# Macaron block on one core: the opening loads most tokens behind the first routing weights, moves the low halves of the weights to POOL, and lets ScalarE normalise three groups whole

## The reference

```python
x = L0_attn_x                                        # (8, 1024, 128) float32
x = x + 0.5 * _L0_ffn_ref(_layernorm(x), Wg, bias_corr, W1, W2, Ws1, Ws2)
x = x + _L0_attn_ref(_layernorm(x), Qw, Kw, Vw)
x = x + 0.5 * _L0_ffn_ref(_layernorm(x), Wg, bias_corr, W1, W2, Ws1, Ws2)
```

```python
scores = sigmoid(flat @ Wg.T)                        # 16 experts in 4 groups
topk_idx, topk_w = _route(scores, bias_corr)         # best 2 groups, best 4 experts, weights normalised, x 2.5
hid = _relu2(einsum('th,eih->eti', flat, W1))        # 16 experts of 64 hidden units
y = einsum('eti,ehi->eth', hid, W2)
out = einsum('eth,te->th', y, cw) + _relu2(flat @ Ws1.T) @ Ws2.T
```

## Time and profile before

| | |
|---|---|
| median of 3 runs | 702.88 us (702.61 to 703.27) |
| profiled execution | 702.95 us |
| its span in the profile | 701.2 us |
| PE busy, of the span | 96% |
| DVE, ACT, POOL busy | 81%, 76%, 62% |
| feed-forward groups in a phase | 16 |

### The profile page before, as it was taken

The page is one execution under the profiler, slowest core; times in us unless marked ns, Lnnn a source line. Parts: engine busy times, 40 slices in busy tenths (PEclk is TensorE's granted clock), DMA queues, the critical chain, the costliest instruction groups (busy, mean ns, idle before and its releaser), DMA issues.

```text
span 701.2 us, 15091 instructions
## 1 busy us (share of the span) xinstructions
PE 673.3 (96%) x3367; PEld 527.5 (75%) x3367; DVE 567.5 (81%) x2586; ACT 529.6 (76%) x1094; POOL 438.2 (62%) x346
## 2 busy tenths in 40 slices
PE   4799999999999997999999999999999999999997
PEld 4567878888788875787778777778788887888775
DVE  5898998899888985666656678898988998889863
ACT  3578888888888866675566477659888788887875
POOL 3379888998889972000000021148889898898875
PEclk9999999999999999999999999999999999999999
DMA  9856776567765640000000000365776787767782
GB/s 246 196 124 138 162 165 145 124 147 154 162 143 123 152 90 0 1 1 1 0 1 0 0 0 1 71 134 115 158 166 140 166 179 171 165 139 174 166 178 72
DMA packets 53525, 78.37 MB, mean 112 GB/s; under 512 B 5216, under 2 KB 19184, under 8 KB 53488
## 3 DMA queue, kind: packets, MB, share of 16 engines
q1 hardware_dynamic: 51280, 77.36, 50.4%
q10 hardware_dynamic: 2208, 0.59, 0.4%
HBM read 72.70 MB, written 5.24 MB: 111 GB/s over the span
## 4 chain that ended last, share of the span: by engine, by line
PE 78%; DVE 10%; ACT 5%; issue 3%; POOL 1%; DMA 1%; POOLq 0%; DVEq 0%; ACTq 0%
PE psum L1188 18%; PE psum L1190 18%; PE psum L1189 18%; PE psum L1397 7%; PE psum L1227 4%; PE psum L1249 4%; DVE nmax L1068 3%; PE psum L1219 2%; PE psum L1261 2%; PE psum L1386 2%; ACT shared L611 2%; PE psum L1410 2%; DVE zn L1082 1%; DVE s_sb L939 1%; ACT wb L446 1%
## 5 line engine op out<-in xcount | busy, mean ns | idle before, releaser
L379 POOL TENSOR_TENSOR shared_r<-shared,shared_r 128x512 fp32r<-128x512 f32 x256 | 325.9, 1294 | 55.6 <-ACT shared L505 53.5
L939 DVE SCALAR_TENSOR_TENSOR s_sb<-psum,wb 128x512 f32<-128x512 f32 x256 | 175.5, 687 | 46.2 <-PE psum L1190 25.9
L505 ACT ACTIVATE shared<-s_sb 128x512 f32<-128x512 f32 x288 | 178.1, 620 | 28.6 <-DVE s_sb L939 28.6
L504 ACT ACTIVATE shared_r<-s_sb 128x512 fp32r<-128x512 f32 x256 | 159.8, 624 | 45.3 <-DVE s_sb L939 43.5
L1188 PE MATMUL psum<-x_hi,w_hi 128*128 128x512 f32 x288 | 127.2, 442 | 1.0 <-DVE x_sb L1094 0.5
L1190 PE MATMUL psum<-x_hi,w_lo 128*128 128x512 f32 x288 | 114.3, 397 | 0.0
L1189 PE MATMUL psum<-x_lo,w_hi 128*128 128x512 f32 x288 | 113.5, 394 | 0.0
L1188 PE MATMUL psum<-shared_r,w_hi 128*128 128x512 f32 x256 | 109.5, 428 | 0.8 <-POOL shared_r L379 0.7
L1189 PE MATMUL psum<-shared_r,w_hi 128*128 128x512 f32 x256 | 101.2, 395 | 0.0
L1190 PE MATMUL psum<-shared_r,w_lo 128*128 128x512 f32 x256 | 101.0, 395 | 0.0
L362 POOL TENSOR_TENSOR a_rstd<-a_mv,neg_half 128x8 f32<-128x8 f32 x8 | 13.1, 1636 | 116.4 <-DVE a_mv L758 116.4
(11 more groups left out here) (166 smaller groups left out, 1301.5 us busy)
## 6 DMA issues: line engine op xcount, KB each, us to landing
wb<-scratch SPq DMA_DIRECT2D x128, 512.0 KB, 8.3
out<-x_sb SPq DMA_DIRECT2D x16, 256.0 KB, 9.8
x_sb<-in_L_attn_x SPq DMA_DIRECT2D x4, 256.0 KB, 6.1
scratch<-wT SPq DMA_DIRECT2D x32, 32.0 KB, 1.9
w_raw<-in_L_ffn_W ACTq DMA_DIRECT2D x1, 512.0 KB, 5.8
w_raw<-in_L_ffn_W SPq DMA_DIRECT2D x1, 512.0 KB, 6.7
w_raw<-in_L_ffn_Ws ACTq DMA_DIRECT2D x1, 64.0 KB, 8.6
w_raw<-in_L_ffn_Ws SPq DMA_DIRECT2D x1, 64.0 KB, 7.2
```

The source lines that it names most:

```text
L379: nc.gpsimd.tensor_tensor(g_lo[:, j % RING, :], g_f[:, j % RING, :], g_hi[:, j % RING, :].bitcast(F32), ALU.subtract).then_inc(F.glo_done, 1)
L504: nc.scalar.activation(g_hi[:, j % RING, :], s_sb[:, j % RING, :], ACT.Square)
L505: nc.scalar.activation(g_f[:, j % RING, :], s_sb[:, j % RING, :], ACT.Square).then_inc(F.sq_done, 1)
L939: ins = nc.vector.scalar_tensor_tensor(s_, h_, 0.0, wb[:, u, c, :], ALU.max, ALU.mult)
```

## The change

It touches the opening alone, and the loads of tokens that belong to it.

- The first 4 tiles come in two DMAs, one from SP and one from ACT. ACT issues the loads of `W2` and `Ws2` only when both have landed.
- Group 4 has a DMA of its own, behind `Qw`, `Kw` and `Vw`. Groups 5 and 6 (512 KB) are issued behind the four `wb` loads of group 0, and groups 7 to 15 (2.36 MB) behind those of group 1. DVE waits for the former ahead of the loop's first body and for the latter ahead of the hardware loop.
- `weights_lo` goes from DVE to POOL. POOL can't read PSUM, so ACT writes an unrounded copy of each set as well (`wt_f`, in `zn` and `oT`).
- ACT normalises groups 1, 2 and 3 whole (four tiles in place of two), and DVE only makes their `shift`.
- PE gets 32 transposes of the identity whose result nobody reads (`keep_busy`), the first `w_transpose` goes ahead of the fourth set of weights, and PE waits for two low sets ahead of the first `up` and for all five ahead of the first `down`.

```diff
@@ block.sync
-            sp.dma_start(x_sb[:, 0:TG, :], x_v[:, 0:TG, :]).then_inc(x_in[0], 16)
+            sp.dma_start(x_sb[:, 0:TG // 2, :], x_v[:, 0:TG // 2, :]).then_inc(x_in[0], 16)
...
-            sp.dma_start(x_sb[:, 4 * TG:NT, :], x_v[:, 4 * TG:NT, :]).then_inc(x_rest, 16)
             sp.dma_start(qk_raw[:, 0, :], Qw).then_inc(small_in, 16)
             sp.dma_start(qk_raw[:, 1, :], Kw).then_inc(small_in, 16)
             sp.dma_start(vw[:], Vw).then_inc(small_in, 16)
+            sp.dma_start(x_sb[:, 4 * TG:5 * TG, :], x_v[:, 4 * TG:5 * TG, :]).then_inc(x_in[4], 16)
...
                 for n in range(2 * UN):
                     spread(n, n % UN)
+                    if phase == 0 and n < 2:
+                        cs = slice(TG * XR[n], TG * XR[n + 1])
+                        sp.dma_start(x_sb[:, cs, :], x_v[:, cs, :]).then_inc(x_rest[n], 16)
@@ block.gpsimd, start
                     if F is FF[0]:
                         x_lo_part(0, 0)
+                        weights_lo(0)
                         norm_root(0)
                         inv(2)
+                        weights_lo(1)
...
+                    if F is FF[0]:
+                        weights_lo(2)
+                    inv(3)
                     x_lo_part(1, 1)
-                    inv(3)
                     norm_root(1)
+                    if F is FF[0]:
+                        weights_lo(3)
+                        weights_lo(4)
@@ block.scalar
+            sc.dma_start(x_sb[:, TG // 2:TG, :], x_v[:, TG // 2:TG, :]).then_inc(x_in[0], 16)
+            sc.wait_ge(const_done, 1)
+            nc.scalar.activation(warm[:], neg_half[:], ACT.Sigmoid)
+            sc.wait_ge(x_in[0], 32)
             sc.dma_start(w2_raw[:, 0:NC, :].rearrange("h c (j i) -> h (c j) i", i=I),
...
                     sigmoid(0, 0, lg_ps)
-                    first_half(1)
+                    whole_group(1)
                     x_hi_copy(0, 0)
                     weights_hi(0)
                     x_copy(1, 1, tr_ps)
                     weights_hi(1)
                     sigmoid(1, 1, lg_ps)
                     weights_hi(2)
+                    wT_copy(0, wT_ps)
                     weights_hi(3)
                     x_hi_copy(1, 1)
-                    wT_copy(0, wT_ps)
-                    first_half(2)
+                    whole_group(2)
...
-                    first_half(3)
+                    whole_group(3)
@@ weights_hi
                 if w < 2:
-                    copy(flat(w1_hi, w), src).then_inc(wt_hi, 1)
+                    copy(flat(w1_hi, w), src)
+                    copy(wt_f[w], src).then_inc(wt_hi, 1)
@@ block.vector, opening
                     statistics(1)
-                    second_half(1)
+                    norm_shift(1)
...
-                    weights_lo(0)
-                    weights_lo(1)
-                    second_half(2)
+                    route_parts(1, 0, 1)
+                    norm_shift(2)
@@ block.tensor
+                def keep_busy(times):
+                    for n in range(times):
+                        nc.tensor.transpose(wt_ps[4][:, 0:P], ident[:], ident[:])
...
                     pe.wait_ge(const_done, 2)
+                    keep_busy(20)
                     pe.wait_ge(wg_in, 16)
                     nc.tensor.transpose(lg_ps[:, 0:E], wg_raw[:], ident[0:E, 0:E]).then_inc(wgT_done, 1)
+                    keep_busy(12)
...
                     pe.wait_ge(wt_hi, N_SETS)
-                    pe.wait_ge(wt_lo, N_SETS)
+                    pe.wait_ge(wt_lo, 2)
```

More of the change, by code:

```diff
@@ L222, in macaron_kernel @@
         uT = s_sb[:, AHEAD:AHEAD + 2, :]
+        zn_flat = zn[:].rearrange("p u t d -> p (u t d)")
+        wt_f = [zn_flat[:, 512 * w:512 * (w + 1)] for w in range(4)] + [oT[:]]
         psum = ctx.enter_context(nc.psum_tensor("psum", [P, 8, 512], F32))
@@ L256, in macaron_kernel @@
         N_SETS = len(wt_ps)
-        x_in = [sem(f"x_in{g}") for g in range(4)]
-        x_rest = sem("x_rest")
+        x_in = [sem(f"x_in{g}") for g in range(5)]
+        x_rest = [sem(f"x_rest{n}") for n in range(2)]
+        XR = (5, 7, NG)
         wg_in, bias_in, w1_in, w2_in, small_in = sem("wg_in"), sem("bias_in"), sem("w1_in"), sem("w2_in"), sem("small_in")
@@ L365, in attention_inv, with weights_lo @@
                 inv_std(AT, b, a_mv[:, :, 1], a_rstd[:], [(AT.zn_done, 2 * b)])
+            def weights_lo(w):
+                pool.wait_ge(wt_hi, w + 1)
+                flat = lambda a, k: a[:, 4 * k:4 * k + 4, :].rearrange("p c n -> p (c n)")
+                lo_of = lambda lo, hi, f: nc.gpsimd.tensor_tensor(lo, f, hi.bitcast(F32), ALU.subtract)
+                if w < 2:
+                    lo_of(flat(w1_lo, w), flat(w1_hi, w), wt_f[w]).then_inc(wt_lo, 1)
+                elif w < 4:
+                    lo_of(flat(w2_lo, w - 2), flat(w2_hi, w - 2), wt_f[w]).then_inc(wt_lo, 1)
+                else:
+                    lo_of(w1_lo[:, NC, :], w1_hi[:, NC, :], wt_f[w][:, 0:P])
+                    lo_of(w2_lo[:, NC, :], w2_hi[:, NC, :], wt_f[w][:, P:2 * P]).then_inc(wt_lo, 1)
             def ffn(F):
@@ L450, in _ @@
             sc.dma_start(w2_raw[:, NC, :], Ws2).then_inc(w2_in, 16)
-            sc.wait_ge(const_done, 1)
-            nc.scalar.activation(warm[:], neg_half[:], ACT.Sigmoid)
             def normalise(F, g, t):
@@ L509, in first_half, with whole_group @@
                         normalise(F, n, t)
+                def whole_group(n):
+                    for t in range(TG):
+                        normalise(F, n, t)
                 def opening():
@@ L688, in weights_hi @@
                             copy(w2_f[:, n, :], src[:, (c % 4) * P:(c % 4 + 1) * P])
-                    copy(flat(w2_hi, w - 2), src).then_inc(wt_hi, 1)
+                    copy(flat(w2_hi, w - 2), src)
+                    copy(wt_f[w], src).then_inc(wt_hi, 1)
                 else:
@@ L692, in weights_hi @@
                     copy(w2_hi[:, NC, :], src[:, P:2 * P])
+                    copy(wt_f[w][:, 0:2 * P], src[:, 0:2 * P])
                     copy(qkT[:].rearrange("p c n -> p (c n)"), src[:, 2 * P:4 * P]).then_inc(wt_hi, 1)
@@ L724, in _ @@
             v.wait_ge(FF[0].stat, n_const)
[L726 to L737, removed]
             def carry(place):
@@ L960, in statistics @@
                     def statistics(n):
-                        v.wait_ge(x_in[n], 16)
+                        v.wait_ge(x_in[n], 32 if n == 0 else 16)
                         stats(n, range(TG))
@@ L972, in opening @@
                     route_parts(0, 9)
-                    weights_lo(0)
-                    weights_lo(1)
-                    second_half(2)
+                    route_parts(1, 0, 1)
+                    norm_shift(2)
                     statistics(3)
[L977 to L980, removed]
-                    route_parts(1, 2)
-                    weights_lo(4)
-                    route_parts(1, 3, 4, 5, 6, 7, 8)
-                    v.wait_ge(x_rest, 16)
+                    route_parts(1, 2, 3, 4)
+                    norm_shift(3)
+                    route_parts(1, 5, 6, 7, 8)
+                    v.wait_ge(x_in[4], 16)
                     for c in range(AHEAD):
@@ L1040, in run @@
                 def run(first_extra, last_extra):
+                    if phase == 0:
+                        v.wait_ge(x_rest[0], 16)
                     body(0, True, False, first_extra)
+                    if phase == 0:
+                        v.wait_ge(x_rest[1], 16)
                     if phase == 1:
@@ L1246, in down @@
                         wait(pe, F.oT_copied, g - 1)
+                        if phase == 0 and isinstance(g, int) and g == 0:
+                            pe.wait_ge(wt_lo, N_SETS)
                     if c in WHOLE:
@@ L1277, in opening @@
                     weights_transpose(2)
+                    w_transpose(0, wT_ps, sigmoids=2)
                     weights_transpose(3)
-                    w_transpose(0, wT_ps, sigmoids=2)
                     pe.wait_ge(F.xf_done, 2)
```

## The result

The changed kernel takes 709.97 us (median of 5, 708.01 to 711.98), the kernel before 703.27 us beside it (median of 5, 702.61 to 703.68). The ratio is 1.0096, with a 95% interval of 1.0073 to 1.0118: slower by 6.7 us. The forecast was 709.0 us. Two numbers limit how finely this may be read. The executions of the changed kernel lie 4 us apart, those of the kernel before 1 us. And the profiled execution of the change took 711.27 us (span 709.5), 1.3 above its median. So the traces say where time goes, and the medians say how much.

A forecast was written before the change was run, and what follows sets the result against it. The prediction took PE as the bound, its opening set by the chain with ACT: 702.95 + 3.0 for the opening + 2.9 for the moved tokens = 708.85, stated as 709.0 us, range 704.3 to 711.5 (about 0.85).

The forecast's parts named there:

- the opening: Start of the kernel, up to the first gate: a longer chain of ACT and PE costs +3.0 us.
- the stall: Gate of group 2: it waits 4.5 us for `wb`, and PE loses 2.9 us.
- Step 1: PE's start: 32 added transposes at 0.22 us each end at 8.9, so the first transposes of tokens come +0.5 us.
- Step 1's clock: PE in the opening: the sum keeps it at its slow level, 1.2 GHz, despite the added transposes.
- its rival: PE in the opening: added transposes bring the fast clock and some 5.2 us back, total 704.8; chance 0.13.
- Steps 2 to 4: ACT's added tiles and copies in the opening: `x_copy(1)` +1.1, fourth high set +2.0, group 3 +3.5, first `up` at 33.2.
- DVE's possible delay by POOL's subtractions: Routing of group 0 in the opening: 0 to +1.8 us possible beside POOL's five subtractions, taken as none.
- Step 5: First gate in the opening: from 31.54 to 35.0, +3.4 us, less the 0.49 DVE had stood for POOL's root.
- The moved tokens: SP's queue: store 2 waits behind 36 tiles, landing at 60.2; group 2's gate comes 4.5 late, PE loses 2.9 us.
- the store does not wait: SP's queue: the store is not held up by the tokens, only the opening counts, total 706.0; chance 0.15.
- the ledger: SP's stores and loads timed in order: tokens landed at 59.8, store 2 at 60.2, first half of group 2's `wb` at 68.4.

The follow-up runs named there:

- E1: The change with the load of `Ws2` issued by SP, behind that of `Ws1`, instead of by ACT: 707.67 us against 703.18 for the kernel before.
- E4: The kernel before with the 32 added transposes and nothing else: 702.26 us against 703.18.
- E9: The kernel before with first tokens in two DMAs, `Ws2` on SP, token loads redivided, 28 transposes at the start and 38 in PE's later waits: 700.34 us against 703.04.
- E11: E9 with only the 28 added transposes at the start, without the 38 in PE's later waits: 701.75 us, ratio 0.9983 to the kernel before.
- E10: E9 without any added transposes, only the order of its loads left: 702.93 us against 702.87 for the kernel before.
- E5: The change without its 32 added transposes: 711.81 us against 703.04 for the kernel before.
- E7: The kernel before with the moved tokens and nothing else: 707.72 us against 703.04.
- E3: The change with `Ws2` issued by SP and the tokens of groups 5 to 15 loaded in the opening: 704.64 us against 703.18 for the kernel before.
- E8: E3 with DVE normalising two tiles of groups 1, 2 and 3 again: 703.12 us against 703.04 for the kernel before.
- E2: The change with the tokens of groups 5 to 15 loaded in the opening, behind group 4: 706.69 us against 703.18 for the kernel before.

## Why the prediction was right, and where its steps were off

The time and its side were right, by the mechanism it named: a longer chain of ACT and PE, and a store held up by the tokens. How near it came is luck. The sum was made for the profiled execution, 708.85, and that took 711.27: it should have read 4.8 for the opening, 2.5 for the stall and 0.8 later, where it read 3.0, 2.9 and nothing. That the median lies 1.3 below this execution brought the forecast within 1 us of it.

*Step 1, the first transposes of tokens: +0.5, measured +2.4.* This is the mis-sized term. The step priced the added transposes on PE (8.9) and asked only when the tiles land. It left out that ACT issues two DMAs between the landing and its first tile, though the edit moves them there. One of them held ACT 5.87 us. E1 shows it: 2.2 us by the medians. Without the hold the tokens come at 7.95, even ahead of the 8.44 of before, because the added transposes end at 8.1 and not at 8.9.

*Step 1's clock, and its rival: wrong in the mechanism, right in most of its effect.* The sum had PE slow throughout, since "the rows lean to the second" of the two answers that it quoted. The 12 transposes from 6.36 took 1.67 us, which is the fast level, and the clock column falls to 0.51 between 10 and 20. The added transposes do bring 2.4 GHz, and the change had lost it by the time PE had stood 2.83 us. The Trainium skill, TensorE: Matmul & The Clock Gate, Part 4, says that the fast clock does not engage for transposes; E1, E4, E9 and E11 contradict it: 0.60 to 0.66 us for the first four token transposes behind the added ones. Part 1 of the same page of the Trainium skill, by which activity of the array releases the clock, agrees with these. My reason against was that twelve transposes in a row from 12.03 had changed nothing; that one stretch was no evidence on another, as E10 shows, where PE turned fast on tokens, logits and weights alone. What the rival priced at 5.2 us is worth 0.9 on the kernel before and 2.6 in E9 (against E10), and in the change perhaps 2.1, which isn't clear of its spread. It is less than priced since the clock falls again within the opening and other engines hold part of the gain.

*Steps 2 to 4, the extra work on ACT: right.* With step 1's error taken off, they can be checked one by one. From the sigmoid to `x_copy(1)` the step gave 3.25 us and the trace has 3.13. The fourth high set was to come 1.5 later than by step 1 alone and came 4.08 - 2.42 = 1.7 later. The first `up` was to move 3.5 - 0.5 = 3.0 further and moved 5.48 - 2.42 = 3.06. DVE's possible delay by POOL's subtractions was rightly taken as nothing in the opening: from the sigmoid of group 0 to its `scw` it is 6.97 us before and after. It comes in the second phase instead. Where the hold happened to be smaller, in E5, the first `up` is at 32.22 against the forecast's 33.2.

*Step 5, the first gate at 35.0 with several us of DVE idle: measured 36.95 with 6.82.* It took the 0.49 us off that DVE had stood for POOL's root behind the gate, and rightly: `scw` followed at once, so of +5.41 for the gate +4.84 is left.

*The moved tokens: right in each step.* The store was to need 6.3 us to land (53.9 to 60.2) and needed 5.9; the gate was to wait 4.5 and waited 3.90; PE was to lose 2.3 to 3.5, taken as 2.9, and lost 2.5 in the trace, 3.2 by the medians. So "the store does not wait" is out. E1, E5 and E7 add a point that the ledger implied: the stall grows as the opening shrinks (3.3, 4.1 and 4.3 us by `scw`, where the change has 2.5), so part of the opening's loss is paid only once. It isn't in strict step, as the opening of E5 is later than that of E1.

*The last 0.8 us* was in no step; the text ahead of the prediction says that the change touches the opening alone. Most of it is the 0.7 us of the moved `inv(3)` in the second phase: DVE slowed beside POOL's subtraction, which the prediction priced for the opening (up to 0.6 for an operation of DVE) and took as nothing. Its price came from ACT's pair; DVE's own pair takes 0.60 us alone, at 25.98 before, so the 1.48 beside the subtraction meant 0.9. Another 0.3 us comes up to the first `scw` of the second phase. The other kernels lose 0.1 (E4, E5, E10) to 0.8 us (E3) at that place, also those that gain in the opening, as E9 (0.65); that cause stays open.

Not settled is how the 1.4 us between E3 and E8 reaches the end, and how the last 1.0 between E8 and E4 divides; no run took its parts singly.

## What to carry to other kernels

When a DMA is moved on an engine that also computes, price the issue itself on that engine, not only the transfer: here 0.4 us for one and up to 5.87 for the next. A small store whose reader is on the path must not stand behind a large load of the same issuer; divide the load so that a piece fits in each gap between stores. Work taken off an engine buys nothing if it goes onto the chain that the others wait for: here DVE ended with 6.82 us to spare and the first gate came 5.4 us later. And a line moved in a function that two phases share changes both: read the second phase's trace as well.

## What the runs showed of the hardware that was not expected

- PE reaches its fast level on transposes whose result nobody reads: 20 in 4.53 us, then 12 in 1.67 (0.22 and 0.12 each). It also does so on real work alone: in E10 eight logits take 1.06 us at 14.41, where the kernel before still needs 1.89 at 15.52.
- The wait just ahead does not tell by itself whether PE is still fast. It was after waits up to 1.25 us in E1, and it was slow behind 1.96 us in E1 (1.06 for four) and behind 2.10 in E11 (1.08 for four at 19.77, where E9, with that time filled, has 0.63). But E9 turned slow at about 22 us although its last waits were 0.73 and 0.69 us, and E2 was fast behind a wait of 3.03 us and slow only at the next step, at 11.56:

```profile
10.12 0.66 PE L1240 MATMUL psum<-ident,xn 128*128 128x128 f32 x4 [3.03 <-ACT xn L488]
```

- The granted-clock column reads 1.00 at the head of a trace while PE is slow by its durations (and E5, 1.00 up to 35 us with 1.95 for eight transposes). It fell to 0.50 only in kernels where PE had first been fast. Trust the durations there.
- Issuing `Ws2` behind `W2` held ACT for 2.35 to 5.87 us; issued by SP in E1, the same load took 0.43. The Trainium skill, DMA: Bandwidth & Descriptors, section Issuing engines are not separate DMA queues, calls the issue usually small relative to the DMA; for this one the trace does not agree: in the change the issue is 5.87 of the 11.1 us from issue to landing.
- DVE's `shift` of 128x4 elements took 0.85 us beside POOL's 128x512 subtraction and 0.15 us without it.
